# Moving the head sums of a first cross attention to GpSimd, and turning the tail of a second one onto token rows

## The reference

```
x = x + tanh(g_xattn[0]) * L0_xattn(layernorm(x), ctx, ...)   # 16 heads of 64, key j seen by query i only where j % 100 == i
x = x + tanh(g_ffn[0])   * L0_ffn(layernorm(x), ...)          # latent attention, then 8 experts of 128
x = x + tanh(g_xattn[1]) * L1_xattn(layernorm(x), ctx, mask)  # 16 heads of 16 over all 361 keys
x = x + tanh(g_ffn[1])   * L1_ffn(layernorm(x), centroids...) # 8 experts of 684, top 2 by distance to a centroid
```

## Time and profile before

| | us |
|---|---|
| runs of the kernel before | 834.2, 835.34, 839.5 (median 835.34) |
| the profiled execution's own time | 835.02 |
| its span, first to last instruction | 833.2 |
| TensorE busy (share of the span) | 743.4 (89%) |
| DVE busy | 558.7 (67%) |
| ACT busy | 383.8 (46%) |
| GpSimd busy | 179.2 (22%) |
| mean granted TensorE clock | 0.941 |

### The profile page before, as it was taken

The page is one execution under the profiler, slowest core; times in us unless marked ns, Lnnn a source line. Parts: engine busy times, 40 slices in busy tenths (PEclk is TensorE's granted clock), DMA queues, the critical chain, the costliest instruction groups (busy, mean ns, idle before and its releaser), DMA issues.

```text
span 833.2 us, 13395 instructions
## 1 busy us (share of the span) xinstructions
PE 743.4 (89%) x4761; PEld 612.5 (74%) x4761; DVE 558.7 (67%) x1025; ACT 383.8 (46%) x832; POOL 179.2 (22%) x131
## 2 busy tenths in 40 slices
PE   6998899999889569999998898888999699999996
PEld 3577778888865258668995576667765699999995
DVE  3369999998728979747666466766654666656652
ACT  4512222222253239845434365656664445555651
POOL 0012000001003514510003302222321133334432
PEclk9999999999999879988999899998869599999999
DMA  6400000000060000000000866535061248999983
GB/s 235 200 1 19 18 19 19 19 1 1 1 267 21 0 1 2 2 1 0 2 9 27 174 150 151 138 91 173 2 222 68 91 171 285 323 303 300 306 252 63
DMA packets 29048, 85.97 MB, mean 103 GB/s; under 512 B 3887, under 2 KB 19599, under 8 KB 25655
## 3 DMA queue, kind: packets, MB, share of 16 engines
q1 hardware_dynamic: 25143, 79.87, 29.3%
...
## 4 chain that ended last, share of the span: by engine, by line
PE 65%; DVE 18%; issue 8%; ACT 5%; DMA 2%; POOLq 0%; SPq 0%; DVEq 0%; ACTq 0%
PE PS L486 61%; DVE RW L1714 3%; DVE RO L1717 2%; PE PS L1028 1%; DVE WK L1774 1%; DVE SM L2012 1%; DVE WK L1771 1%; PE PS L657 1%; DVE PROD L1670 1%; DMA KST<-mask_rows 1%; DVE SM L1687 1%; PE PS L874 1%; ACT SQ L1073 1%; PE PS L998 1%; DVE RW L1683 1%
## 5 line engine op out<-in xcount | busy, mean ns | idle before, releaser
L486 PE MATMUL PS<-CTXH,WKV0H 128*128 128x362 f32 x256 | 88.4, 345 | 14.0 <-DVE PROD L1670 13.4
L2012 DVE TENSOR_REDUCE SM<-PS 100x1 f32<-100x362 f32 x128 | 64.9, 531 | 47.4 <-PE PS L486 46.5
L486 PE MATMUL PS<-CTXL,WKV0H 128*128 128x362 f32 x256 | 84.6, 330 | 0.0
L486 PE MATMUL PS<-CTXH,WKV0L 128*128 128x362 f32 x256 | 84.5, 330 | 0.0
L1132 ACT COPY RW<-PS 128x361 f32<-128x361 f32 x64 | 29.6, 462 | 90.7 <-PE PS L486 53.7
L1316 ACT ACTIVATE WK<-PS 120x400 f32<-120x400 f32 (+1 forms) x96 | 48.3, 507 | 44.5 <-PE PS L486 43.5
L486 PEld LDWEIGHTS PS<-CTXH,WKV0H 128*128 128x128 f32 x256 | 48.6, 190 | 25.7 <-DVE PROD L1670 18.7
L486 PE MATMUL PS<-KST,QST 97*100 97x362 f32 x128 | 55.2, 444 | 5.7 <-DMA KST<-mask_rows 3.2
L1566 POOL DMA_INDIRECT out<-YO,TROW x20 | 38.3, 1917 | 88.8 <-DMA out<-YO,TROW 63.3
L1717 DVE TENSOR_REDUCE RO<-RW 128x100 f32<-128x400 f32 x64 | 55.9, 873 | 2.2
L486 PE MATMUL PS<-RB,HTT 114*128 114x256 f32 (+1 forms) x240 | 55.3, 379 | 0.6 <-ACT HTT L1415 0.6
...
## 6 DMA issues: line engine op xcount, KB each, us to landing
...
```

The source lines that it names most:

```text
L486: return pe.matmul(out, lhsT, rhs, start=start, stop=stop)
L2012: dve.tensor_reduce(SM1[:, q % 2, j:j + 1], PS[0:S, i % 2, 0:KVE], AX_X, ALU.max, negate=True).then_inc(sem["c_maximum_found"], 1)
```

## The change

Three things are changed in the first cross attention. The sum over four keys leaves DVE: GpSimd adds the halves of `PV` (200 columns) in place and then the two quarters (100 columns) into `OT0`; `PV` has three buffers instead of two. The low part of the context (from batch 2 on) leaves DVE for GpSimd too. The rounding of the attention weights (`SES`, L1699) leaves DVE for ACT, ahead of `vcopy`.

The second one's tail is written anew. Odd groups of heads keep their values in the other half of each 32 rows, so that two groups can be packed into one: DVE copies bank 6 once (`copy_mixed`, at the end of a batch's first iteration), and out of this copy takes the sums (`place_sums`, second iteration) and the values (`pack_values`, third), and divides (`divide`, fourth); GpSimd has no part in it. The output product has tokens on its rows, with 264 columns: 256 of x and 8 for the centroids (`WO1`, scaled by the gate); two more products in the same bank add x itself by an identity (`TURNER`), also multiplied by the centred centroids. `project_out(b)` for batches 0 to 5 is put into the last four iterations of the quad loop. ACT copies the rows out (`copy_tokens`), DVE takes mean and variance per row (`statistics`), ACT normalises the rows. The fourth layer norm, the transposes, the squares and the router products fall away. Biases are folded beforehand (`fold_output`, `fold_centroids`, and the additions to X by GpSimd).

The diff, cut to its core:

```diff
             def mix_v(q):
...
                     if b > 0:
-                        pe.wait_ge(sem["c_mixed_copied"], 2 * b)
+                        pe.wait_ge(sem["c_mixed_copied"], b)
+                if (b, g) == (4, 0):
+                    fold_output()
+                if (b, g) == (5, 0):
+                    fold_centroids()
...
+            def project_out(b):
+                rows_free(b)
+                pe.wait_ge(sem["c_mixed_divided"], b + 1)
+                out = PS[0:S, ROWBANK[b], 0:264]
+                for c in range(2):
+                    mm(out, OT1[:, c, tok(b)], WO1[:, c, :], c == 0, False)
+                mm(out[:, 0:136], X[:, 0, tok(b)], TURNER[:, 8:144], False, False)
+                mm(out[:, 128:264], X[:, 1, tok(b)], TURNER[:, 0:136], False, True).then_inc(sem["c_output_summed"], 1)
...
+                if q in (28, 29):
+                    project_out(q - 28)
+                if q in (30, 31):
+                    project_out(2 * q - 58)
+                    project_out(2 * q - 57)
...
+            def round_weights(b):
+                act.wait_ge(sem["a_weights_ready"], b + 1)
...
+                act.copy(SES[:, b % 2, :], SE[:, 1, :]).then_inc(sem["a_probs_high_ready"], 1)
...
-                act.wait_ge(sem["c_mixed_copied"], 2 * b + 1)
+                act.wait_ge(sem["c_sums_placed"], b + 1)
                 act.activation(SUMS, SUMS, ACT.Ln).then_inc(sem["c_sums_inverted"], 1)
...
+            for b in (3, 4, 5):
+                copy_tokens(b)
             invert_sums(B - 1)
-            add_bias("c_output_summed", 0, 2, 1, "c_output_gated", [WK[:, i, :] for i in range(4)])
-            norm(5)
+            copy_tokens(6)
+            act.wait_ge(sem["c_statistics_found"], B)
+            act.activation(RSTD, MOMENTS[:, :, 1], ACT.Ln, bias=COLS[0:S, 15:16]).then_inc(sem["norm_log_taken"], 1)
...
+            copy_tokens(7)
             act.preload_act_table_set("sqrt_and_others")
...
+            for b in range(B):
+                act.activation(ROWS[:, b, :].rearrange("p (k c) -> p k c", k=KD), RESID[:, b, :, :], ACT.Identity, bias=SHIFTS[:, b:b + 1],
+                               scale=RSTD[:, b:b + 1]).then_inc(sem["rows_copied"], 1)
...
+            def add_keys(b):
+                for ti in range(TI0):
+                    i = TI0 * b + ti
+                    pool.wait_ge(sem["a_weighted"], i + 1)
+                    pv = PV[:, i % 3, :]
+                    pool.tensor_tensor(pv[:, 0:2 * S], pv[:, 0:2 * S], pv[:, 2 * S:4 * S],
+                                       ALU.add).then_inc(sem["a_halves_added"], 1)
+                    pool.wait_ge(sem["a_halves_added"], i + 1)
+                    pool.tensor_tensor(OT0[:, ti, tok(b)], pv[:, 0:S], pv[:, S:2 * S],
+                                       ALU.add).then_inc(sem["a_heads_mixed"], 1)
...
-                    if i > 1:
-                        dve.wait_ge(sem["a_heads_mixed"], i - 1)
+                    if i > 2:
+                        dve.wait_ge(sem["a_heads_mixed"], i - 2)
...
-                    dve.tensor_reduce(OT0[:, ti, tok(b)], PV[:, i % 2, :].rearrange("p (c i) -> p i c", c=NC),
-                                          AX_X, ALU.add).then_inc(sem["a_heads_mixed"], 1)
...
+                dve.tensor_copy(MIXED, PS[:, 6, 0:4 * S]).then_inc(sem["c_mixed_copied"], 1)
+
+            def place_sums(b, mixed):
...
+                link(dve.tensor_scalar(pair(OPPOSITE), mixed[:, :, 0, :], UPPER, None, ALU.mult))
+                link(dve.scalar_tensor_tensor(pair(OPPOSITE), mixed[:, :, 1, :], LOWER, pair(OPPOSITE), ALU.mult, ALU.add))
+                dve.stream_shuffle(SUMS, OPPOSITE, [q ^ 16 for q in range(32)]).then_inc(sem["c_sums_placed"], 1)
...
-                if g == 1 and b >= 1:
-                    outs(b - 1)
...
+                if b >= 1:
+                    if g == 0:
+                        copy_mixed(b - 1)
+                    if (b, g) == (5, 0):
+                        centre_centroids()
+                    if g == 1:
+                        place_sums(b - 1, sides(MIXED))
+                    if q == 29:
+                        dve.wait_ge(sem["c_values_summed"], 2 * B)
+                        gu_low(0, 0)
+                    if g == 2:
+                        pack_values(b - 1, sides(MIXED))
+                    if g == 3:
+                        divide(b - 1)
+            for b in (0, 1, 2):
+                statistics(b)
+            dve.wait_ge(sem["c_heads_mixed"], 4 * B)
+            place_sums(B - 1, sides(PS[:, 6, 0:4 * S]))
+            pack_values(B - 1, sides(PS[:, 6, 0:4 * S]))
+            statistics(3)
+            divide(B - 1)
+            for b in (4, 5, 6, 7):
+                statistics(b)
```

376 lines of the change are left out of this document (218 added, 158 removed).

## The result

The changed kernel takes **810.95 us** (median of four, 809.94 to 813.27) against 835.24 (834.2 to 839.5) for the kernel before, run beside it: a ratio of 0.9704, 95% interval 0.9664 to 0.9743. It is faster by 24.3 us. I had forecast 789 with a range of 774 to 806, so the direction was right, the size wrong by 22 us, and the range did not hold it.

The account below looks back on a forecast made before the run. DVE's lag behind TensorE was taken to bound the first attention, bank-6 waits and low clock the quad loop, a five-engine chain the tail; -18 - 8.5 - 19.7 = -46.2 on 835.02 gave 789 us, range 774 to 806.

Parts of the forecast that it names:

- The warning that DVE's products might be blocked: First cross attention: GpSimd's additions block DVE operations with one operand in PSUM, 861 us; chance 0.03.
- GpSimd sets the pace: First cross attention: at 2 us a tile GpSimd bounds the phase, the saving falls to 6 us, 801 us; chance 0.15.
- Term A: First cross attention: with sums off DVE, TensorE sets the phase; -18 us, bounds -10 and -22.
- the last batch: First cross attention, batch 7: DVE's 1.44 us a tile falls to TensorE's 1.2, saving 1.9 us.
- The stages between: Untouched code between the changed parts: taken as constant, its times as in the one profile used.
- Term B: Second cross attention's quad loop: stall and low clock go, output products and folds are added; -8.5 us, bounds -18 and +1.
- The stall: Quad loop: one earlier copy of bank 6 removes TensorE's 1.58 us wait before a batch's first `mix_v`; -10.5 us.
- The clock: Quad loop and after: TensorE's granted clock rises as the stalls go, winning back 9 of 11.5 us.
- The folds: Quad loop: 12 small TensorE products that fold the biases beforehand add 2.9 us.
- the quad loop gives nothing back: Quad loop: DVE's new steps wait for masks, the clock still falls, output products cost in full; +1, 799 us; chance 0.17.
- Term C: Tail behind the last `mix_v`: a chain of 7.8 us replaces 27.5 before routing; -19.7 us, bounds -21.5 and -14.
- what follows stays: Tail from routing to the first expert block: unchanged, 11.7 us to the token list and 6.5 to the block.

Follow-up runs that it names:

- gu_early: Changed kernel with DVE's `gu_low(0, 1)` issued behind the first three statistics instead of behind `route`: 805.51 us, ratio 0.9665.
- before_again: The kernel before without any edit, profiled a second time: 835.43 us.
- bc_only: Changed kernel with the first cross attention as in the kernel before: 822.56 us, ratio 0.9814.
- dve_order: Changed kernel with DVE's new quad-loop steps issued between the third and fourth maximum of an iteration, not behind the split: 807.74 us, ratio 0.9666.
- outs_early: Kernel before with only the two reads of bank 6 moved an iteration earlier, between the third and fourth maximum: 826.35 us, ratio 0.9867.

## Why the prediction was wrong, point by point

**What bounds the first attention: right.** TensorE's floor of 19.8 us a phase was measured at 19.75, the waits for the products went, and GpSimd's additions were forecast at 0.61 and 0.39 us and took 0.615 and 0.401. The warning that DVE's products might be blocked did not come true. The rival "GpSimd sets the pace" is refuted.

**Term A, the sum: -18 forecast, -14.1 in the profile, -10 to -15 timed.** The six phases gave 12.4 us of the 13.8 (one of them had 0.9 us more than the others). The step that failed is the last batch: I took its 1.44 us a tile for DVE's pace and expected 1.9 us, where 0.7 came. The spreads of batch 7 lie from 197.25 to 207.08 us, 9.8 us as before: TensorE never stopped in it, and both kernels ran some three microseconds of it at half clock behind the wait for the first spread. In gu_early, the same code there at full clock, they took 8.3 us. That pace was the clock's, not DVE's. The step before it gave 0.5 of 1.4 us, the first phase 0.4 of 1. Part by part the misses are about 1.4 us (phases), 1.2 (last batch), 0.9 (step before it) and 0.6 (first phase).

**The stages between, held to move as a whole: 4.3 us lost between the two profiles.** I forecast differences from one execution and took the untouched stages as a constant. They vary by 5 us from one execution to the next with the clock (before_again, bc_only). This is a fault of the comparison, not a cost of the change: the mean of the profiles gives 13.6 us at the first scores. In the medians it is contained and can't be taken apart.

**Term B: -8.5 forecast, -0.7 in the profile. This is the step that failed most.** The loop itself kept its length. Four parts:
- The stall, forecast -10.5. It went by name, but TensorE's idle time fell by only 5.5 us. I wrote that what follows on DVE (`top`) has slack of a quad. It has none: TensorE writes the scores of a quad into two banks by turns, and waits for the maximum two products back. 1.2 us of new steps ahead of two maxima came out in 0.67 + 0.54 us of waits, and over the loop the waits for the maxima and the keys' low part are 5.7 us for 0.8. dve_order (the slot alone, for the changed kernel's steps) and outs_early (the slot alone, for the old reads) show that the slot decides.
- The clock, forecast -9. The time lost, an estimate by length x (1 - granted clock), went from 14.6 to 6.6 us: -8.0. It counts idle time too and so is rather too large. Against the second profile of the kernel before (11.7) it is -5.
- The output products, +8.2: one in the loop took 1.43 us (1.37 forecast).
- The folds, +2.9: 3.1 us of products in the trace, with the wait of 0.7 us ahead of them.

By these parts the loop should have become some 2 us shorter (-5.5 - 8.0 + 8.6 + 3.1); it did not, and this rest is not placed.

The second rival, "the quad loop gives nothing back", had 0.17. Its number, +1, is near what happened, but its mechanism is not: DVE's steps came in the way of maxima, not of masks, and the clock did not fall all the same, it rose from 0.89 to 0.95. The untested assumption was that the one copy removes the stall; the slot alone takes 9.8 us (8 to 15) off the median of the kernel before, without touching the tail.

**Term C: -19.7 forecast, -14.8 measured.** The chain was right (7.0 us for 7.8). The step that failed is "what follows stays", with `gu_low(0, 1)` "under the gather's 6.5". I had put the 3 us of DVE's work beside the gather as hidden, although the same text had the rule that DVE's work on two SBUF operands and a GpSimd instruction keep each other waiting; and I had looked at when the fourth load is wanted, not at what it is issued beside. Together +4.3. Another +1.35 is the half clock at the placing products, where TensorE is busy for only 9.56 of the 24 us from 616 on.

Counted up against the forecast: +3.9 (A), +4.3 (between), +7.8 (B), +4.9 (C) and 0.3 at the end make 21 of the 22 us. My range had two rivals together at its upper end, 806; it held no case in which several small losses meet, and none for the untouched stages.

**What stays open.** Why the clock falls at one pause of 1.4 us in one execution and not in the next was not found. Nor was it settled why the moved order of DVE's steps loses behind batch 4 what it won before: from there the distances are 18.2, 17.3 and 17.0 us in dve_order and 19.5, 16.2 and 14.9 in the changed kernel.
